# SyncE fetches one edge tile per round by single-row transfers; GpSimd gathers 12 tiles fewer

## The reference, cut to what matters

```python
# x: [6250, 128], src, dst: [200000] (sorted by dst), edge_attr: [200000, 64], all fp32 / int32
msg  = relu(x[src] + edge_attr @ We + be)            # one message for each edge
aggr = segment_sum(msg, dst, num_segments=6250)
h = (1 + eps) * x + aggr
h = relu(h @ W1 + b1) @ W2 + b2
h = (h - mean(h, 0)) * rsqrt(var(h, 0) + 1e-5) * gamma + beta     # batch norm over the nodes
out = layernorm(x + relu(h) + x)
```

## Time and profile before

| | us |
|---|---|
| median of 3 runs | 1559.09 (1558.66 to 1559.86) |
| the profiled execution, its own time | 1564.18 |
| its span, from the first to the last instruction | 1562.2 |
| PE busy in it | 1416.0 (91%) |
| ACT busy | 1255.7 (80%) |
| POOL busy | 1160.5 (74%) |
| DVE busy | 891.9 (57%) |

### The profile page before, as it was taken

One profiled execution on the slowest core, in us unless ns is written; L12 is line 12 of the kernel. 1 busy time (PEld: TensorE's weight loads), 2 busy tenths in 40 slices (PEclk: granted clock), 3 DMA queues, 4 the chain that ended last, 5 costly groups with the idle time before them and its releaser, 6 DMA issues.

```text
span 1562.2 us, 60471 instructions
## 1 busy us (share of the span) xinstructions
PE 1416.0 (91%) x23435; PEld 1095.0 (70%) x23435; DVE 891.9 (57%) x3174; ACT 1255.7 (80%) x3729; POOL 1160.5 (74%) x1193
## 2 busy tenths in 40 slices
PE   1299999999999999989999999989999999999954
PEld 1277777777777777767777777767777777777734
DVE  5676665655566565555555556555556555655436
ACT  2488888888888888878877888878788888888845
POOL 7677777777777777777777777777777777777762
PEclk9999999999999999999999999999999999999967
DMA  9644445444544445444444444445444444444432
GB/s 250 170 111 109 109 113 123 113 111 117 119 113 110 108 112 126 109 106 113 111 108 106 113 106 113 112 106 117 108 110 107 111 112 107 105 112 110 104 125 84
DMA packets 148516, 180.72 MB, mean 116 GB/s; under 512 B 41725, under 2 KB 128980, under 8 KB 147972
## 3 DMA queue, kind: packets, MB, share of 16 engines
q1 hardware_dynamic: 102489, 89.62, 24.5%
q0 software_dynamic: 37728, 77.31, 20.9%
q10 hardware_dynamic: 8011, 9.90, 2.3%
HBM read 170.09 MB, written 6.63 MB: 113 GB/s over the span
## 4 chain that ended last, share of the span: by engine, by line
PE 55%; POOL 21%; issue 8%; ACT 5%; DVE 4%; DMA 4%; SPq 1%; ACTq 0%; POOLq 0%; DVEq 0%
POOL xg L590 21%; PE ps L1396 20%; PE ps L1381 14%; PE ps L1325 9%; PE ps L1311 6%; DMA xg<-xb,idxb 3%; ACT hot L747 2%; ACT msg L753 1%; PE ps L1362 1%; ACT hot L740 1%; PE ps L1342 1%; PE ps L1365 1%; PE ps L1334 1%; PE ps L1337 1%; SPq L480 1%
## 5 line engine op out<-in xcount | busy, mean ns | idle before, releaser
L590 POOL DMA_INDIRECT xg<-xb,idxb x1145 | 1107.0, 967 | 356.9 <-issue 337.0
L1396 PE MATMUL ps<-iota_all 128*128 128x128 bf16 x8064 | 518.0, 220 | 0.0
L1396 PEld LDWEIGHTS ps<-iota_all 128*128 128x128 bf16 x8064 | 452.3, 98 | 87.1 <-issue 67.7
L984 DVE TENSOR_TENSOR msg<-ps,xg 128x512 f32<-128x512 f32 x390 | 264.5, 688 | 305.6 <-DMA xg<-xb,idxb 192.8
L707 ACT ACTIVATE iota_all<-ps 128x384 bf16<-128x384 f32 x896 | 379.8, 484 | 31.7 <-PE ps L1381 28.4
L740 ACT ACTIVATE hot<-iota,rel 128x64 f32<-128x64 f32 x1560 | 391.6, 339 | 0.0
L1381 PE MATMUL ps<-x,iota_all 112*32 112x384 bf16 x7168 | 365.1, 331 | 0.0
L1069 DVE TENSOR_TENSOR accT<-accT,ps 128x64 f32 x390 | 86.2, 221 | 292.4 <-PE ps L1342 248.1
L753 ACT ACTIVATE msg<-msg 128x512 f32<-128x512 f32 x390 | 241.0, 618 | 14.7 <-DVE msg L984 14.7
L1381 PEld LDWEIGHTS ps<-x,iota_all 112*32 112x32 bf16 x7168 | 156.9, 96 | 120.6 <-issue 38.5
L1325 PE MATMUL ps<-msg,hot 128*64 128x128 f32 x3120 | 219.4, 284 | 23.1 <-ACT msg L753 23.1
(11 more groups left out here) (145 smaller groups left out, 800.3 us busy)
## 6 DMA issues: line engine op xcount, KB each, us to landing
ea<-in_eat SPq DMA_DIRECT2D x156, 320.0 KB
lowB<-lowD SPq DMA_DIRECT2D x128, 224.0 KB
xg<-xb,idxb POOLq DMA_INDIRECT x1145
accT<-in_xt ACTq DMA_DIRECT2D x1, 3125.0 KB, 14.8
x<-in_xt ACTq DMA_DIRECT2D x1, 3125.0 KB, 11.0
out<-iota_all SPq DMA_DIRECT2D x5, 512.0 KB
iota_all<-in_x ACTq DMA_DIRECT2D x3, 784.0 KB, 17.6
xb<-iota_all SPq DMA_DIRECT2D x3, 784.0 KB, 16.8
```

The lines of the kernel that those rows point to most:

```text
L590: pool.indirect_dma_start(out=xg[0:rows, slot, j, :], out_offset=None, in_=of, in_offset=bass.IndirectOffsetOnAxis(ap=index, axis=0)).then ...
L984: add = dve.tensor_tensor(both, lin_of(half), xg[:, g % RING, :, :].rearrange("p (b t) h -> p b (t h)", b=2), ALU.add)
L1396: last = pe.matmul(found[:, e, :], sel2[set_of(k)][:, t, e * P:(e + 1) * P], rows3[:, t, a, :], start=(t == 0 and e == 0 and a == 0), stop ...
```

## The change

Of one group per round (`FETCH_G` = 3, in the rounds 1 to 12) GpSimd gathers three tiles instead of four. The 128 rows of the fourth tile are fetched by SP during the round before, each by a DMA of its own of 1 x 128 fp32 from `xb` to one partition of a new buffer `xs` (two halves, for even and odd rounds). SP reads the row numbers from a buffer `idxs` in SBUF into registers, nine at a time, and issues nine transfers behind the lows of each of the 15 pairs (two behind the last). The numbers of the tile are loaded one round ahead by one DMA. In the fetched group DVE waits for the 128 transfers and makes three adds (128, 128 and 256 columns) in place of one of 512. `g_msg`, which only a branch that isn't taken here uses, moves to another buffer.

```diff
+    FETCH_G = 3
+    FETCH_ROWS = 9
...
+        def fetched(i, g):
+
+            return i > 0 and g == FETCH_G
+
         def by_pool(i, g):
 
-            return GROUP - HALF * special(i, g)
+            return GROUP - HALF * special(i, g) - fetched(i, g)
...
+            def load_sources(i):
+
+                e0 = (i * ROUND + FETCH_G) * GE + (GROUP - 1) * P
+                sp.dma_start(idxs[:, i % 2, :], src_row[:, e0:e0 + P]).then_inc(s_idxs, 16)
+
+            def fetch(i, a, b):
+
+                if a == 0:
+                    wait_apart(sp, s_idxs, 16 * i)
+                    if i == 1:
+                        for m in range(NQ):
+                            sp.wait_ge(s_xb[m], stores(m))
+                    if i >= 3:
+                        wait_apart(sp, s_pre, (i - 2) * ROUND + FETCH_G + 1)
+                _, node_of = nc.values_load_multi_w_load_instructions(
+                    idxs[0:1, i % 2, a:b], engines=[mybir.EngineType.SP], min_val=0, max_val=N - 1,
+                    skip_runtime_bounds_check_because="each is the src of an edge, a row of x")
+                for p in range(a, b):
+                    sp.dma_start(xs[p:p + 1, i % 2, :], xb[bass.ds(node_of[p - a], 1), :]).then_inc(s_row[i % 2], 16)
...
                     for j, k in phase(i, q, 3):
                         spread_lows(j, k)
-
+                    if i + 1 < ITERS:
+                        fetch(i + 1, q * FETCH_ROWS, min(P, (q + 1) * FETCH_ROWS))
+                    if q == STEPS - 1 and i + 2 < ITERS:
+                        load_sources(i + 2)
+
+            load_sources(1)
...
+                if fetched(i, g):
+                    dve.wait_ge(s_row[i % 2], 16 * P * ((i + 1) // 2))
+                    dve.tensor_tensor(to[:, 3, :], ps_lin(half, 3), xs[:, i % 2, :], ALU.add)
+                    dve.tensor_tensor(to[:, 2, :], ps_lin(half, 2), xg[:, g % RING, 2, :], ALU.add)
+                    add = dve.tensor_tensor(to[:, 0:2, :].rearrange("p t h -> p (t h)"), lin_of(half)[:, 0, :],
+                                            xg[:, g % RING, 0:2, :].rearrange("p t h -> p (t h)"), ALU.add)
+                else:
+                    both = to.rearrange("p (b t) h -> p b (t h)", b=2)
+                    add = dve.tensor_tensor(both, lin_of(half), xg[:, g % RING, :, :].rearrange("p (b t) h -> p b (t h)", b=2),
+                                            ALU.add)
```

More of the change, by code:

```diff
@@ L100, in gine_layer_kernel @@
     CLOSE = 11
+    FETCH_G = 3
+    FETCH_ROWS = 9
+    assert FETCH_ROWS * STEPS >= P and FETCH_G not in SORTED
     BANKS = (3, 7, 4)
@@ L238, in gine_layer_kernel @@
             .rearrange("p (t a h) -> p t a h", t=NTILE, a=3)
+        xs = sb("xs", [P, 2, HID])
+        idxs = sb("idxs", [1, 2, P], i32)
         g_idx = sb("g_idx", [P, 1], i32)
@@ L241, in gine_layer_kernel @@
         g_xg = sb("g_xg", [P, HID])
-        g_msg = sb("g_msg", [P, HID])
+        g_msg = iota_all[:, N + 22:N + 22 + HID]
         g_dst = sb("g_dst", [P, 4])
@@ L300, in gine_layer_kernel @@
         s_last = sem("s_last")
+        s_idxs = sem("s_idxs")
+        s_row = [sem("s_row_even"), sem("s_row_odd")]
         s_pro = sem("s_pro")
@@ L982, in add_x @@
                 to = msg[:, q % TURN, half * GROUP:(half + 1) * GROUP, :]
-                both = to.rearrange("p (b t) h -> p b (t h)", b=2)
-                add = dve.tensor_tensor(both, lin_of(half), xg[:, g % RING, :, :].rearrange("p (b t) h -> p b (t h)", b=2),
-                                        ALU.add)
+                if fetched(i, g):
[8 more added lines that the diff above has]
+                                            ALU.add)
                 if isinstance(i, int) and i == 0 and g < UNBIASED:
```

## The result

| | before | after |
|---|---|---|
| median of 4 runs, us | 1558.88 (1557.72 to 1559.86) | 1792.2 (1790.6 to 1795.36) |
| the profiled execution | 1564.18 | 1790.6 |
| its span | 1562.2 | 1788.8 |
| PE, ACT, POOL busy | 91%, 80%, 74% | 83%, 71%, 64% |

The ratio is 1.150, with a 95% interval of 1.148 to 1.152. The forecast was 1753 us, slower, with SP as the new bound.

A forecast was written before the change was run, and what follows sets the result against it. GpSimd's gather stream (112.5 us a round) was taken as the bound, with SP at 130 us replacing it: profiled 1564.2 + 214 - 20 = 1758 us, median 1753 us, 12% slower; range 1542 to 1870.

The forecast's parts named there:

- The gathers: On GpSimd: twelve gathers fewer at 1.25 us each save 15.0 us; DVE's three adds costed at nothing.
- A row: On SP: each single-row transfer costs 0.33 issue + 0.05 gap + 0.04 register instruction, 0.42 us; 128 rows 54 us.
- The loads: On SP: register loads at 0.22 us a register, read from DVE's 2.25 us gap, 28 us a round (18 to 37).
- SP's old work: On SP: existing issues and unavoidable landing waits use 48 us a round, leaving about 64 us for new work.
- The round: On SP: 48 + 54 + 28 + 0.3 = 130 us per fetching round, against GpSimd's 112.5, or 111.3 with 89 gathers.
- the sum over the rounds: Rounds 0 to 11 lose 12 x (130.3 - 112.5) = 214 us; round 12 gives back 20, leaving 194 us.
- The 15 us by which SP may be late: On SP: about two pairs of lateness before DVE lacks lowB or TensorE ea; used up in the first round.
- the forecast's correction from the profiled execution to the median: Whole kernel: the profiled execution took 5.1 us more than the median, so 1758 us profiled gives median 1753.
- The rival in which the new work fits: SP's sum stays under 111 us (low ends 102), gathers' 15 us come in full, 1544 us; chance 0.27.
- The rival of the transfers as the limit: In SP's queue: single-row transfers finish one after another, 1.3 us each, 166 us a round, 2181 us; chance 0.03.
- The rival of lateness in neighbouring pairs: SP fits on average but lows are late where batches follow; decides above 4.3 us per nine-row fetch; 1562 to 1600 us; 0.06.
- the floor of about 600 ns for a register load: On SP: if a load's whole price, 15 x 0.6 = 9 us a round, and SP would be just within its time.

The follow-up runs named there:

- the kernel that has nothing else: Changed kernel with the fetched tile brought by one 128 x 128 transfer a round, no register reads; twelve fewer gathers and three adds kept: 1542.68 us.
- in eights: Changed kernel with eight rows behind each pair and twelve behind pairs 5 and 11, so every load starts at a multiple of four: 1640.94 us.
- the kernel with fixed rows: Changed kernel with the same 128 single-row transfers a round, but from constant addresses, without register loads or register arithmetic: 1542.34 us.
- the half fetch: Changed kernel with one tile fetched only every second round, five rows a pair, six gathers fewer than before: 1551.56 us.
- the two kernels there: Changed kernel with fetch between lowD and lowB, two lowD halves, numbers loaded earlier: 1556.27 us; that kernel with seven or twelve rows a pair: 1555.19 us.
- a fetch that fits: Kernel with fetch between lowD and lowB and two lowD halves, given eight rows a pair, twelve in pairs 5 and 11: 1543.17 us.

## Why the prediction was right, and where its sizes were off

The mechanism held in each step that the runs could test (the gain of the gathers, the sum of SP's own time as the pace, nothing else that costs), and the measured time lies in the range. Several sizes were off, and some of them cancel.

- **The gathers.** 15.0 us forecast, 16.1 measured by the kernel that has nothing else (15.2 with the mean distance of 1.27 us). DVE's three adds: nothing, as forecast.
- **A row.** 0.42 us forecast, 0.41 measured, though by parts that differ: the issue of a single row is 0.23 us, not the 0.33 of the small tiles in the earlier trace rows, and register work and gaps are 0.18 (0.037 and 0.029 us of instructions and gaps of 0.04 between them), not 0.09. That the sum came out is luck.
- **The loads.** 28 us a round forecast, 25.4 measured. The gap of 2.25 us in the earlier trace rows was indeed the load, which itself took 2.30 us (outside the 1.43 to 2.25 that were read from the gap), but it is one of the slow half. A constant price for a register was the wrong shape: the price hangs on where a load begins, and the same 128 numbers took 11.4 us a round in eights. That 25.4 came near 28 is because most of the nines begin badly.
- **SP's old work.** 48 us forecast; 129.9 less 52.5 for the rows (128 x 0.41) and 25.4 for the loads leaves 52, in which landings are 23.7 (284.6 us over 12 rounds).
- **The round.** 130.3 us forecast, 129.9 to 130.2 measured.
- **What was mis-sized is the sum over the rounds.** The same `lowD`, the first behind the last fetch, is issued at 1408.77 before and 1643.25 after; the one ahead of the first fetch at 80.27 and 80.70. So those twelve rounds took 1328.5 us before, 110.7 each and not the 112.5 of 90 gathers, since GpSimd is already ahead when they begin (it issues 1047 gathers in them, not 1080); the difference is 234 us and not 214. And the last round gave back 7.9 us (153.4 to the end of the span before, 145.5 after) and not 20: the 23.9 us of DVE's waits for gathers are gone from it, but its waits for TensorE (the products and the turned windows) grew from 27.2 to 46.2 us. The 15 us by which SP may be late, which the forecast names and takes off nowhere, would show in the same place; they were not taken apart. Start, rounds and last round, 0.4, 20 and 12 us, are 33 of the 39 us between 1753 and 1792. The rest is the forecast's correction from the profiled execution to the median, 5.1 us off before, where the changed kernel's profiled execution was 1.6 us under its median.

The rival in which the new work fits failed by the sum alone: it was 19 us a round away, and 12.3 of them hung on the choice of nine rows instead of eight. Its low end for a load (0.14 us a register) was still above what a load of eight from a multiple of four costs (0.72 us, 0.09 a register). The rival of the transfers as the limit is refuted by the kernel with fixed rows. The rival of lateness in neighbouring pairs asks for a sum near 111 us, which the changed kernel doesn't have; the kernel with fixed rows shows that nine rows ahead of the lows cost nothing by themselves, and the half fetch, with some 3.3 us a pair (1.27 for the load and 5 x 0.41), lies below the 4.3 us from which the rival was to decide. Whether lateness costs something near 111 us stays open: in the two kernels there DVE waited for `lowB`, 73.8 and 27.2 us, and they differ by about 1 us, which is within the noise.

On the floor of about 600 ns for a register load (the Trainium skill, "DMA: Bandwidth & Descriptors", Latency and other measured facts): the trace agrees in size only, with 0.65 us for two registers and 0.72 for eight from a multiple of four. It is no floor here, since twelve loads of four registers took 0.49 to 0.51 us, and nine registers from another start took 2.06. The other figure, about 200 ns a register even in bulk ("Runtime: NRT & Kernel Launch" of the Trainium skill, Instruction fetch mechanics), is given on that page for loads from HBM that the runtime puts around a kernel; these read SBUF. The trace has the same slope for them, 0.2 us for each number of a load that begins elsewhere, and 0.2 us for each four of one that begins at a multiple of four.

What stays open: why the start decides, beyond the count of steps; what held the round at 110.5 us in the two kernels before the last; and the granted TensorE clock, 0.929 of full speed on average against 0.981, which fell with TensorE's gaps, and whose own share in the 233 us was not taken apart (TensorE has 9% of the chain).

## What to carry to other kernels

Work moved to an engine that "only issues DMAs" needs a budget like any other: its instructions, its register loads and the waits that it must sit out, all in one order, against the pace of the loop. Take away the gain and the cost one at a time: here the gain (16 us) was real, and a fetch that fits returns nearly all of it (14.6 us with the right rows). Read each instruction's own duration in the trace where it stands there, and look at shortest, median and longest before taking one number: the two prices of a load were in the trace of the kernel before. When a wait is filled with work, look for what that work was hiding where it stood before.

## What the runs showed of the hardware

- A load of registers from SBUF on SP: nine int32 take 0.91 to 1.17 us from a start at a multiple of four numbers, and 2.05 to 2.31 us from others; eight take 0.72 and twelve 0.95 to 1.01 (medians) from such starts, and twelve 2.66 from others. Two take 0.66 from number 126, and four 0.50 from a multiple of four. On DVE ten take 1.06 to 1.09 and 2.30 to 2.31 us.
- A DMA of one row of 512 bytes is issued by SP in 0.23 us (median), `lowD` of 28 rows in 0.32 and `lowB` of 128 in 0.35; with the row number in a register two more instructions (0.037 and 0.029 us) and their gaps bring a row to 0.41 us.
- `lowD` (28 rows) landed 1.0 us after its issue where only rows stood ahead (822.68) and 4.3 us after it right behind two transfers of `ea` (811.68).
- 128 transfers of single rows a round changed nothing for the others: with the same packets in the queue the kernel was as fast as with one transfer (1542.34 and 1542.68 us).
